# A recurrent layer beside a mixture of experts on one core: another order of the work in each step

## Chip, core and metric

The kernel runs on one NeuronCore of a Trainium2 chip. The metric is the device time of one execution in microseconds (us); lower is better. All data is float32.

## What is computed

`x` holds 32 sequences of 256 tokens with 128 channels, 8192 tokens. Both branches read the same normalised `xn`, and the output joins them:

```python
xn = _layernorm(x, axis=-1)
s = _L0_attn_ref(xn, ...)                 # recurrent branch
g = _silu(_L0_ffn_ref(xn, ...))           # shared expert + one of 8 routed experts
x = x + s * g
```

The recurrent branch is an RWKV layer. Time mixing: layernorm, a blend of each token with the one before it, three products `k`, `v`, `r`, and a recurrence over time with a running maximum:

```python
out = (e1 * aa + e2 * vv) / (e1 * bb + e2)
...
rwkv = sr * _wkv(time_decay, time_first, k, v)
x = x + jnp.einsum('btd,cd->btc', rwkv, att_ow)
h = _ln(x, ln2_w, ln2_b)                  # channel mixing from here
kk = jnp.square(jax.nn.relu(jnp.einsum('btc,fc->btf', xk, f_kw)))
kv = jnp.einsum('btf,cf->btc', kk, f_vw)
x = x + jax.nn.sigmoid(jnp.einsum('btc,dc->btd', xr, f_rw)) * kv
```

The other branch is `silu(x @ wg.T) * (x @ wu.T) @ wd.T` with shared weights for every token, plus the same form with the weights of the token's best expert, applied to `x` times the sigmoid of the best logit.

## The kernel before

Each engine (TensorE, ScalarE, VectorE, GpSimd, and SyncE for transfers) has a program of its own, written out by hand in one order; engines meet at semaphores that count finished instructions. An instruction that waits holds up everything behind it on its engine.

The 8192 tokens are 16 chunks of 512. A prologue loads and normalises all of them, transposes them into `XT` and computes the router's logits. Then come steps 0 to 17. Step `i` works on three chunks: it opens chunk `i+1` (transpose of `z1`, `make_h1`, `make_d1`, `time_mixes`, the products `k`, `v`, `r`, `running_max`, `differences`), does the recurrence of chunk `i` (`decays`, `wkv_b`, `wkv_a`, `den_and_num`, `inverse_of_den`, `make_tn`, `make_rw`), and finishes chunk `i-1` (`attention_out`, `make_x2`, `rstd_of_x2`, `make_z2`, `make_h2`, `channel_mixes`, four `ffn_key` products, relu, square, `ffn_value`, `make_s`). `make_x2` adds the attention output and takes its statistics on VectorE; `rstd_of_x2` makes four instructions of four columns on GpSimd from them; `make_z2` on ScalarE applies them. The inverse of the denominator is `exp(-ln(den + 1))`, and its table of functions is loaded in each step (L735), and the table with tanh and silu again (L749). The square of the keys is made for two quarters on ScalarE and for two on VectorE (L1069). GpSimd makes `rw` (L837).

Between these pieces each step has eight places, `fill(i, 0)` to `fill(i, 7)`, which stand in every engine's order. `plan()` puts other work there:

- `S m q`: half of chunk `m` of the shared expert: two products, silu, a product on VectorE; with `q = 0` also the down product of chunk `m-1`. `D m` is a down product alone.
- `E n`: a slot of the routed experts. A tile has 128 tokens of one expert, and there are 71. Slot `n` does gate and up of tile `n` (8 matmuls, L486), transposes tile `n+2` (1), and does down of tile `n-2` (4, L500). SyncE loads a tile's 384 KB of weights into one of five buffers, when the down product of the tile five before it is done.
- `Z c`: the final part of chunk `c`: add shared and routed rows, silu, times the recurrent branch, plus `x`, store. It needs all experts.

Steps 0 to 5 hold the shared chunks 0 to 13 (step 0 eight halves, the others four each). Before the experts, GpSimd must scatter all 64 tiles of tokens into expert order in DRAM, by indirect transfers: four in step 0 and twelve in each of the steps 1 to 5. Steps 6 to 14 hold the experts, eight slots a step. Step 15 holds Z 0 to 5, step 16 the shared chunks 14 and 15 and Z 6 to 12, and step 17 the last four.

In a step of before, TensorE ends with key 0, key 1, `k`, `v`, key 2, key 3, `r` and the whole value product, so that all of chunk `i-1` ends in step `i`.

## Time and profile before

| | |
|---|---|
| device time, median of 3 | 577.74 us (577.66 to 578.63) |
| the profiled execution | 577.9 us, of which the span of instructions is 576.1 |
| TensorE busy | 464.0 us (81%) |
| VectorE busy | 425.2 us (74%) |
| ScalarE busy | 345.6 us (60%) |
| GpSimd busy | 264.7 us (46%) |
| mean granted TensorE clock | 0.959 |
| `attention_out` of a step starts | 100.0 (step 1), 127.6, 155.9, 183.0, 210.1, 237.2 (step 6), 269.7, 298.2, 327.4, 355.9, 384.7, 413.2, 441.7, 470.4 (step 14), 497.3, 531.8 |

`attention_out` opens a step on TensorE, so that the differences of the last row are the lengths of the steps. In rows of the trace, L12 is line 12 of the kernel, PE is TensorE's matmuls, PEld its weight loads, DVE VectorE, ACT ScalarE, POOL GpSimd and SPq the queue of transfers. Each fp32 matmul of the program stands there as two instructions. `[0.61 <-DMA ...]` is idle time of the engine before the instruction, and what ended it.

### The profile page before, as it was taken

What the parts mean: (1) busy time and instruction counts of PE and PEld (TensorE: products, weight loads), DVE (VectorE), ACT (ScalarE), POOL (GpSimd) and SP (SyncE); (2) the same over time, 40 slices, a digit from 0 to 9 for tenths busy, and PEclk for the clock granted to TensorE, in tenths of its full rate; (3) what the DMA queues carried; (4) which work ended last, traced back from release to release, by engine and by line L of the source; (5) the groups of instructions that cost most, each with busy time, mean ns of one, the idle gap of its engine ahead of it and who ended that gap; (6) DMA issues with size and microseconds to landing.
All of it is one profiled execution on the core that took longest, in us unless ns stands there. A gap on an engine that the chain in (4) does not pass through costs nothing. (4 is left out here: it accounts for less than half of the span.)

```text
span 576.1 us, 8950 instructions
## 1 busy us (share of the span) xinstructions
PE 464.0 (81%) x2623; PEld 345.9 (60%) x2623; DVE 425.2 (74%) x836; ACT 345.6 (60%) x707; POOL 264.7 (46%) x317
## 2 busy tenths in 40 slices
PE   0989777797979797889898989898989897637661
PEld 0989244564646464787777777777777776425341
DVE  3553795879697977695969596969696968783766
ACT  3776423665646566676776677677777676536441
POOL 6664003657575858461818181818181828210100
PEclk9999988999899999999999999999999999957986
DMA  6329404010000001262727282727272825245482
GB/s 200 110 75 257 96 0 155 22 36 26 33 25 33 31 27 38 62 186 73 221 71 211 84 222 73 209 85 220 73 225 71 226 66 167 73 136 158 128 236 73
DMA packets 68864, 64.97 MB, mean 113 GB/s; under 512 B 5952, under 2 KB 57025, under 8 KB 68816
## 3 DMA queue, kind: packets, MB, share of 16 engines
q1 hardware_dynamic: 63344, 54.31, 34.5%
q0 software_dynamic: 4320, 8.53, 4.2%
q10 hardware_dynamic: 1152, 1.56, 0.8%
q8 instruction: 21, 0.34, 0.2%
q14 instruction: 27, 0.22, 0.1%
HBM read 46.86 MB, written 17.97 MB: 113 GB/s over the span
## 5 line engine op out<-in xcount | busy, mean ns | idle before, releaser
L849 POOL DMA_INDIRECT routed_out<-xh,xs x71 | 91.3, 1286 | 30.2 <-ACT xh L689 16.1
L486 PE MATMUL bank_ring<-xh,ew 128*128 128x128 f32 x568 | 78.6, 281 | 19.9 <-DMA ew<-ex_w 9.3
L486 PEld LDWEIGHTS bank_ring<-xh,ew 128*128 128x128 f32 x568 | 68.8, 191 | 26.9 <-ACT xh L689 15.2
L841 POOL DMA_INDIRECT tokens_by_expert<-xn,pos x64 | 67.2, 1051 | 37.0 <-issue 18.5
L1069 DVE TENSOR_TENSOR kk<-rk 128x512 f32<-128x512 f32 x32 | 26.3, 822 | 54.3 <-ACT rk L650 54.3
L689 ACT ACTIVATE xh<-bank_ring 128x256 f32<-128x256 f32 (+1 forms) x75 | 27.8, 371 | 63.4 <-PE bank_ring L500 62.3
L440 PEld LDWEIGHTS bank_out<-fvw,kk 128*128 128x128 f32 x512 | 60.9, 195 | 8.2 <-issue 8.2
L440 PE MATMUL bank_out<-fvw,kk 128*128 128x128 f32 x512 | 60.8, 278 | 0.0
L823 POOL TENSOR_SCALAR x_sm<-x_mv 128x4 f32<-128x4 f32 x16 | 3.8, 235 | 111.8 <-DVE x_mv L1051 111.8
L470 PE MATMUL bank_ring<-xt,sup 128*128 128x512 f32 x64 | 34.9, 628 | 17.5 <-DVE hs L1085 10.6
L837 POOL TENSOR_TENSOR rw<-den_num,lq 128x512 f32<-128x512 f32 x16 | 20.3, 1269 | 53.8 <-issue 46.5
L500 PE MATMUL bank_ring<-ew,hx 128*128 128x128 f32 x284 | 43.5, 276 | 0.7 <-DVE hx L1093 0.7
L449 PEld LDWEIGHTS bank_ring<-sdn,hs 128*128 128x128 f32 x256 | 31.6, 196 | 15.8 <-DVE hs L1085 12.0
L500 PEld LDWEIGHTS bank_ring<-ew,hx 128*128 128x128 f32 x284 | 38.1, 194 | 1.0 <-ACT xh L689 0.9
L1093 DVE TENSOR_TENSOR hx<-px,bank_ring 128x256 f32<-128x256 f32 x71 | 29.0, 408 | 13.1 <-ACT px L692 12.9
L431 PE MATMUL bank_fa<-xk,fkw 128*128 128x512 f32 x64 | 36.4, 653 | 2.3 <-ACT rk L650 2.3
L449 PE MATMUL bank_ring<-sdn,hs 128*128 128x128 f32 x256 | 32.3, 280 | 6.9 <-DVE hs L1085 6.9
L464 PE MATMUL bank_ring<-xt,sup 128*128 128x512 f32 x64 | 34.9, 628 | 2.3 <-ACT tg L668 2.3
L431 PE MATMUL bank_fb<-xk,fkw 128*128 128x512 f32 x64 | 34.3, 617 | 3.0 <-ACT tf L644 3.0
L1085 DVE TENSOR_TENSOR hs<-tg,bank_ring 128x512 f32<-128x512 f32 x32 | 21.7, 679 | 17.5 <-ACT tg L668 11.8
L470 PEld LDWEIGHTS bank_ring<-xt,sup 128*128 128x128 f32 x64 | 11.4, 193 | 38.7 <-DVE hs L1085 18.0
L572 ACT ACTIVATE xn<-xi,nb,rs 128x128 f32<-128x128 f32 x64 | 26.3, 482 | 12.1 <-POOL nb L801 11.9
(139 smaller groups left out, 1124.0 us busy)
## 6 DMA issues: line engine op xcount, KB each, us to landing
ew<-ex_w SPq DMA_DIRECT2D x71, 384.0 KB, 4.0
xi<-x SPq DMA_DIRECT2D x32, 256.0 KB, 3.7
tokens_by_expert<-pad_row SPq DMA_DIRECT2D x1, 4686.0 KB, 21.2
xs<-tokens_by_expert SPq DMA_DIRECT2D x71, 66.0 KB, 3.6
ew<-routed_out SPq DMA_DIRECT2D x16, 256.0 KB, 3.3
out<-xn SPq DMA_DIRECT2D x16, 256.0 KB, 3.2
routed_out<-xh,xs POOLq DMA_INDIRECT x71, 4.1
tokens_by_expert<-xn,pos POOLq DMA_INDIRECT x64, 2.3
```

The lines of the kernel that those rows point to most:

```text
L431: nc.tensor.matmul((FA, FB)[q % 2][:, :], part(FKW, q, P), XK2[:, :], start=True, stop=True)\
L440: last = nc.tensor.matmul(part(BO, j, CH), KK[:, q * CHUNK + j * P:q * CHUNK + (j + 1) * P], part(FVW, q, CH), start=(q + j == 0), stop=(q ...
L449: last = nc.tensor.matmul(part(b, j, CH), h[:, q * CHUNK + j * P:q * CHUNK + (j + 1) * P], part(SDN, q, CH), start=(q == 0), stop=(q == EQ ...
L464: nc.tensor.matmul(ring(5 * m + 3 * q)[:, :], part(SUP, q, P), part(XT, m, CHUNK), start=True, stop=True)\
L470: nc.tensor.matmul(ring(5 * m + 3 * q + 1)[:, :], part(SUP, EQ + q, P), part(XT, m, CHUNK), start=True, stop=True).then_inc(s_su, 1)
L486: last = nc.tensor.matmul(part(GU[n % 2], q, P), part(w, q, P), xt[:, 0:P], start=True, stop=True)
L500: last = nc.tensor.matmul(BX[:, P:P + CH], part(h, q, P), part(w, 2 * EQ + q, CH), start=(q == 0), stop=(q == EQ - 1))
L572: last = nc.scalar.activation(xn_tile(t), part(XI[c % 4], j, P), ACT.Identity, bias=NB[:, t:t + 1], scale=RS[:, t:t + 1])
L689: nc.scalar.activation(XH[n % NXH][:, a:b], BX[:, a:b], ACT.Copy).then_inc(s_xh, 1)
L841: nc.gpsimd.indirect_dma_start(xs_dram, bass.IndirectOffsetOnAxis(ap=POS[:, t:t + 1], axis=0), XN[:, t * XROW:(t + 1) * XROW], None).then_ ...
L849: nc.gpsimd.indirect_dma_start(routed_dram, bass.IndirectOffsetOnAxis(ap=XS[(n - 2) % NXS][:, CH:CH + 1].bitcast(i32), axis=0), XH[n % NXH ...
L1093: nc.vector.tensor_tensor(HX[n % NHX][:, :], PX[n % 2][:, :], GU[n % 2][:, EF:2 * EF], ALU.mult)\
```

## The change

The plan: experts start at step 5 instead of 6, so that they take steps 5 to 13; the shared chunks 12 to 15 come behind them, into steps 14 and 15, and `D 15` into step 16. Z 0 to 3 go into step 14, Z 4 to 9 into step 15, Z 10 to 15 into step 16, and only Z 16 remains for step 17. GpSimd scatters fifteen tiles a step in steps 1 to 4.

```diff
-EARLY, LATE = 14, 16
-E_STEP = 6
+EARLY, LATE = 12, 16
+E_STEP = 5
...
     late = [("S", m, q) for m in range(EARLY, LATE) for q in range(2)] + [("D", LATE - 1, 0)]
-    for k, item in zip((0, 1, 2, 3, 4), late):
-        steps[CHUNKS][k].append(item)
-    for c in range(6):
-        steps[CHUNKS - 1][c + 2].append(("Z", c))
-    for c in range(6, CHUNKS - 3):
-        steps[CHUNKS][c - 6].append(("Z", c))
-    for c in range(CHUNKS - 3, CHUNKS + 1):
-        steps[CHUNKS + 1][0].append(("Z", c))
+    for n, item in enumerate(late):
+        steps[E_STEP + width + n // 4][2 * (n % 4)].append(item)
+    for c in range(CHUNKS):
+        n = c + 2
+        steps[E_STEP + width + n // 6][1 + n % 6].append(("Z", c))
+    steps[CHUNKS + 1][7].append(("Z", CHUNKS))
...
+        TR = [sb(f"tr{u}", CHUNK) for u in range(2)]
+        X2 = [sb(f"x2{u}", CHUNK) for u in range(2)]
+        KB = (FA, FB, FB, FA)
...
             def key_value(c):
...
                     pe.wait_ge(s_n2, c)
+                    pe.wait_ge(s_ev, c)
...
             def ffn_key(c, q):
                 if q == 0:
                     pe.wait_ge(s_mix2, 2 * c + 2)
-                    pe.wait_ge(s_tr, min(c + 2, CHUNKS))
+                    pe.wait_ge(s_tr, min(c + 3, CHUNKS))
                 elif q == 1:
                     pe.wait_ge(s_tf, c + 1)
+                elif q == 2:
+                    pe.wait_ge(s_rk, 4 * c + 2)
                 else:
-                    pe.wait_ge(s_rk, 4 * c + q - 1)
-                nc.tensor.matmul((FA, FB)[q % 2][:, :], part(FKW, q, P), XK2[:, :], start=True, stop=True)\
+                    pe.wait_ge(s_rk, 4 * c + 1)
+                nc.tensor.matmul(KB[q][:, :], part(FKW, q, P), XK2[:, :], start=True, stop=True)\
                   .then_inc(s_fk, 1)
-            def ffn_value(c):
-                if c > 0:
+            def ffn_value(c, a, b):
+                if a == 0 and c > 0:
                     pe.wait_ge(s_u, c)
-                for q in range(FQ):
-                    pe.wait_ge((s_kk, s_kd)[q % 2], 2 * c + 1 + q // 2)
+                for q in range(a, b):
+                    pe.wait_ge(s_kk, 4 * c + 1 + q)
                     for j in range(TPC):
                         last = nc.tensor.matmul(part(BO, j, CH), KK[:, q * CHUNK + j * P:q * CHUNK + (j + 1) * P],
                                                 part(FVW, q, CH), start=(q + j == 0), stop=(q + j == FQ + TPC - 2))
-                last.then_inc(s_kv, 1)
+                if b == FQ:
+                    last.then_inc(s_kv, 1)
```

`X2` and `TR` have two buffers, so that a chunk's channel mixing can end two steps after its recurrence. The keys 0 to 3 use the banks FA, FB, FB, FA instead of FA, FB, FA, FB, and `v` of a chunk waits also for the `ev` of the chunk before it. The value product comes in two halves, around `attention_out`, with keys 2 and 3 ahead of it; keys and value there are of chunk `i-2`. TensorE's step:

```diff
             def step(i):
                 C, P1 = 0 < i <= CHUNKS, i + 1 < CHUNKS
+                if P1:
+                    z1_transpose(i + 1)
+                if i > 1:
+                    ffn_key(i - 2, 2)
+                    ffn_key(i - 2, 3)
+                    ffn_value(i - 2, 0, 2)
                 if C:
                     attention_out(i - 1)
+                if i > 1:
+                    ffn_value(i - 2, 2, FQ)
+                fill(i, 0)
                 if P1:
-                    z1_transpose(i + 1)
-                fill(i, 0)
+                    key_value(i + 1)
+                if C:
+                    z2_transpose(i - 1)
                 fill(i, 1)
+                if P1:
+                    receptance(i + 1)
                 fill(i, 2)
                 if i == 0:
                     routing_prefix()
                 fill(i, 3)
-                fill(i, 4)
-                if C:
-                    z2_transpose(i - 1)
-                fill(i, 5)
-                fill(i, 6)
                 if C:
                     ffn_receptance(i - 1)
+                    ffn_key(i - 1, 0)
+                fill(i, 4)
+                fill(i, 5)
+                if C:
+                    ffn_key(i - 1, 1)
+                fill(i, 6)
                 fill(i, 7)
-                if C:
-                    ffn_key(i - 1, 0)
-                    ffn_key(i - 1, 1)
-                if P1:
-                    key_value(i + 1)
-                if C:
-                    ffn_key(i - 1, 2)
-                    ffn_key(i - 1, 3)
-                if P1:
-                    receptance(i + 1)
-                if C:
-                    ffn_value(i - 1)
```

ScalarE starts a step with a table load and the inverse of chunk `i-1`, and makes all four squares. The scores of the router are made with Ln and Exp instead of Sigmoid:

```diff
-                nc.scalar.activation(rows_of_xn[:, :, CH + 1], MX[:, :], ACT.Sigmoid).then_inc(s_sc, 1)
+                nc.scalar.activation(SC[:, :], MX[:, :], ACT.Exp, scale=-1.0).then_inc(s_sc, 1)
+                act.wait_ge(s_sc, 1)
+                nc.scalar.activation(SC[:, :], SC[:, :], ACT.Ln, bias=CST[:, K_ONE:K_ONE + 1]).then_inc(s_sc, 1)
+                act.wait_ge(s_sc, 2)
+                nc.scalar.activation(rows_of_xn[:, :, CH + 1], SC[:, :], ACT.Exp, scale=-1.0).then_inc(s_sc, 1)
...
             def step(i):
                 C, T, P1 = 0 < i <= CHUNKS, i < CHUNKS, i + 1 < CHUNKS
-                fill(i, 0)
+                if C:
+                    nc.scalar.preload_act_table_set("natural_log_exp_and_others")
+                    inverse_of_den(i - 1)
+                if i > 1:
+                    ffn_relu(i - 2, 2)
+                    ffn_square(i - 2, 2)
                 if P1:
                     make_h1(i + 1)
+                if i > 1:
+                    ffn_relu(i - 2, 3)
+                    ffn_square(i - 2, 3)
                 if T:
-                    tanh_d(i)
-                fill(i, 1)
+                    decays(i)
+                if i == 0:
+                    scores()
+                if i <= CHUNKS:
+                    nc.scalar.preload_act_table_set("silu_and_others")
+                if i == 0:
+                    tanh_d(0)
+                    receptance(0)
                 if C:
                     make_z2(i - 1)
+                fill(i, 0)
+                if C:
+                    make_h2(i - 1)
+                fill(i, 1)
+                if P1:
+                    receptance(i + 1)
                 fill(i, 2)
                 fill(i, 3)
-                if T:
-                    receptance(i)
-                fill(i, 4)
-                if C:
-                    make_h2(i - 1)
-                fill(i, 5)
-                fill(i, 6)
                 if C:
                     ffn_tanh(i - 1)
+                    ffn_relu(i - 1, 0)
+                    ffn_square(i - 1, 0)
+                fill(i, 4)
+                fill(i, 5)
+                if C:
+                    ffn_relu(i - 1, 1)
+                    ffn_square(i - 1, 1)
+                fill(i, 6)
                 fill(i, 7)
-                if T:
-                    nc.scalar.preload_act_table_set("natural_log_exp_and_others")
-                if C:
-                    ffn_relu(i - 1, 0)
-                    ffn_relu(i - 1, 1)
-                    ffn_square(i - 1, 0)
-                if T:
-                    inverse_of_den(i)
-                if C:
-                    ffn_relu(i - 1, 2)
-                    ffn_relu(i - 1, 3)
-                    ffn_square(i - 1, 2)
                 if P1:
-                    decays(i + 1)
-                if T:
-                    nc.scalar.preload_act_table_set("silu_and_others")
+                    tanh_d(i + 1)
```

GpSimd no longer makes `rw`, and does `make_d1` first:

```diff
             def step(i):
                 C, T, P1 = 0 < i <= CHUNKS, i < CHUNKS, i + 1 < CHUNKS
+                if P1:
+                    make_d1(i + 1)
                 if C:
                     rstd_of_x2(i - 1)
-                if P1:
-                    make_d1(i + 1)
-                for k in range(4):
-                    fill(i, k)
+                fill(i, 0)
                 if 0 < i < E_STEP:
-                    scatter(12)
-                for k in range(4, 8):
+                    scatter(15)
+                for k in range(1, 8):
                     fill(i, k)
                 if i == 0:
                     pool.wait_ge(s_fill, 16)
                     pool.wait_ge(s_rt, RT_PLACED)
-                    pool.wait_ge(s_sc, 1)
+                    pool.wait_ge(s_sc, 3)
                     pool.wait_ge(s_tok, 1)
                     scatter(4)
-                if T:
-                    make_rw(i)
```

VectorE makes `rw`, no squares, and takes `make_s` one step later. `differences`, `wkv_b`, `wkv_a` and `den_and_num` are split, with the same instructions, into `difference_of_key` (the `e2` part), `exp_value` (`ev`), `value_of_now` (`N2`) and `weighted_sums`:

```diff
+            def make_rw(c):
+                dve.wait_ge(s_tn, c + 1)
+                dve.wait_ge(s_iq, c + 1)
+                if c > 0:
+                    dve.wait_ge(s_att, c)
+                nc.vector.tensor_tensor(RW[:, :], NUM, LQ[:, :], ALU.mult).then_inc(s_rw, 1)
...
             def step(i):
                 C, T, P1 = 0 < i <= CHUNKS, i < CHUNKS, i + 1 < CHUNKS
+                if T and i > 0:
+                    value_of_now(i)
+                if i + 2 < CHUNKS and i > 0:
+                    make_z1(i + 2)
                 if C:
+                    make_rw(i - 1)
                     make_x2(i - 1)
+                if P1:
+                    time_mixes(i + 1)
+                if T:
+                    exp_value(i)
                 fill(i, 0)
                 if i == 0:
                     routing_counts()
+                    value_of_now(0)
                 if T:
                     wkv_b(i)
-                fill(i, 1)
+                if i > 1:
+                    make_s(i - 2)
                 if T:
                     wkv_a(i)
-                fill(i, 2)
+                fill(i, 1)
                 if i == 0:
                     routing_starts()
+                if C:
+                    channel_mixes(i - 1)
+                fill(i, 2)
+                if T:
+                    weighted_sums(i)
+                fill(i, 3)
+                if i == 0:
+                    routing_rows()
                 if T:
                     den_and_num(i)
-                fill(i, 3)
-                if P1:
-                    time_mixes(i + 1)
-                if i == 0:
-                    routing_rows()
+                    make_tn(i)
                 fill(i, 4)
-                if C:
-                    channel_mixes(i - 1)
-                fill(i, 5)
-                if T:
-                    make_tn(i)
-                fill(i, 6)
-                if i + 2 < CHUNKS:
-                    make_z1(i + 2)
-                fill(i, 7)
-                if C:
-                    ffn_square(i - 1, 1)
                 if P1:
                     running_max(i + 1)
-                if C:
-                    ffn_square(i - 1, 3)
+                fill(i, 5)
                 if P1:
+                    difference_of_key(i + 1)
                     differences(i + 1)
-                if C:
-                    make_s(i - 1)
+                if i == 0:
+                    make_z1(2)
```

## Rows read from the trace of the kernel before

**Rows 1.** Busy time by stretch (each a step, or several), with its columns

```profile
core 0: us, PE busy (x) PEld busy (x) DVE busy (x) ACT busy (x) POOL busy (x), PEclk, DMA share, GB/s
62.00:100.00 38.00, 27.49 (x95) 14.47 (x94) 28.23 (x50) 15.11 (x23) 6.42 (x6) 0.91 0.21 65
...
100.00:127.60 27.60, 24.15 (x119) 15.26 (x120) 22.49 (x36) 16.95 (x29) 16.85 (x18) 1.00 0.09 30
...
210.10:237.20 27.10, 23.83 (x121) 15.11 (x120) 22.68 (x36) 16.09 (x28) 17.80 (x18) 1.00 0.10 31
237.20:269.70 32.50, 28.39 (x200) 23.35 (x198) 22.77 (x41) 24.11 (x56) 13.75 (x13) 1.00 0.48 134
269.70:298.20 28.50, 25.55 (x177) 20.84 (x176) 22.48 (x40) 20.06 (x46) 14.11 (x14) 1.00 0.52 147
...
441.70:470.40 28.70, 25.30 (x176) 20.77 (x175) 22.50 (x40) 20.05 (x46) 14.80 (x14) 1.00 0.51 146
...
497.30:531.80 34.50, 15.30 (x63) 10.24 (x62) 23.08 (x39) 14.68 (x25) 6.01 (x5) 0.65 0.43 123
531.80:576.10 44.30, 23.16 (x110) 14.29 (x108) 30.62 (x54) 15.44 (x28) 2.57 (x4) 0.86 0.49 142
```

**Rows 2.** A line's group: xcount, busy us, mean ns, idle before and releaser

```profile
L1069 DVE TENSOR_TENSOR kk<-rk 128x512 f32<-128x512 f32 x32 | 26.3, 822 | 54.3 <-ACT rk L650 54.3
```

**Rows 3.** Timeline of an expert step, TensorE: start us, length us, instruction

```profile
328.73 1.06 PE L486 MATMUL bank_ring<-xh,ew 128*128 128x128 f32 x8
...
330.18 1.06 PE L486 MATMUL bank_ring<-xh,ew 128*128 128x128 f32 x8
```

**Rows 4.** Timeline, same step: attention sum, scan, normalisation, table load and inverse

```profile
329.11 0.69 DVE L1044 TENSOR_TENSOR x<-bank_fb,xn 128x512 f32<-128x512 f32 x1
...
331.46 0.24 POOL L823 TENSOR_SCALAR x_sm<-x_mv 128x4 f32<-128x4 f32 x1 [7.78 <-DVE x_mv L1051]
...
332.05 1.22 DVE L1012 TENSOR_TENSOR_SCAN bb_aa<-e 128x514 f32<-128x514 f32 x1
...
333.39 1.65 ACT L629 ACTIVATE z<-x,x_sm 128x128 f32<-128x128 f32 x4
...
346.60 1.28 ACT L735 ACT_TABLE_LOAD   x1
...
349.39 0.72 ACT L620 ACTIVATE lq<-den_num,consts 128x512 f32<-128x512 f32 x1
...
350.14 0.63 ACT L622 ACTIVATE lq<-lq 128x512 f32<-128x512 f32 x1
```

**Rows 5.** Timeline of a shared step, VectorE and GpSimd side by side

```profile
207.27 2.17 DVE L1000 SCALAR_TENSOR_TENSOR e<-pp,vectors 128x512 f32<-128x512 f32 x1
...
207.60 1.28 POOL L837 TENSOR_TENSOR rw<-den_num,lq 128x512 f32<-128x512 f32 x1
209.36 0.73 DVE L1004 SCALAR_TENSOR_TENSOR dd<-pp,vectors,bank_k 128x512 f32<-128x512 f32 x1
```

**Rows 6.** Timeline near the end, VectorE and GpSimd side by side

```profile
536.07 0.68 DVE L1100 TENSOR_TENSOR xn<-xt,xn 128x512 f32<-128x512 f32 x1
536.12 0.72 POOL L824 TENSOR_SCALAR x_sm<-x_mv 128x4 f32<-128x4 f32 x1
```

**Rows 7.** Timeline of the expert step, slots on TensorE and waits for weights

```profile
329.74 0.61 PE L500 MATMUL bank_ring<-ew,hx 128*128 128x128 f32 x4
...
331.18 0.61 PE L500 MATMUL bank_ring<-ew,hx 128*128 128x128 f32 x4
...
334.23 1.13 PE L486 MATMUL bank_ring<-xh,ew 128*128 128x128 f32 x8 [0.61 <-DMA ew<-ex_w]
...
336.82 1.13 PE L486 MATMUL bank_ring<-xh,ew 128*128 128x128 f32 x8 [0.68 <-DMA ew<-ex_w]
```

**Rows 8.** Timeline of step 0: the routing scans, and a slow matmul

```profile
66.92 3.25 DVE L942 TENSOR_TENSOR_SCAN kk<-consts,kk 128x64 f32<-128x64 f32 x8
...
83.73 1.91 PE L464 MATMUL bank_ring<-xt,sup 128*128 128x512 f32 x2
```

81 lines of the change are left out of this document (39 added, 42 removed).

## Prediction

> **What bounds the kernel now.** I read the busy table by stretch first. Before step 1 lie 62 us of prologue and 38 of step 0; then come five shared steps (27.1 us each but for 28.3 once and 27.6 in the first), a first expert step of 32.5, seven of 28.5 to 29.2 that make 200.7 together, one of 26.9, and 78.8 us for steps 15 to 17 [rows 1]. The reader is to see three things. In an expert step TensorE is busy for 25.6 of 28.5 us, VectorE for 22.5 and ScalarE for 20.1: no engine is full, and TensorE has at most 3 us to give. In step 15 TensorE is busy for 15.3 of 34.5 us, and its granted clock is 0.65 [rows 1]. And VectorE stands idle for 54.3 us ahead of its 32 squares, waiting for ScalarE's relu [rows 2]. So before, the end of a step is a chain of key, relu, square and value product on which everything waits. The change cuts it in two and lays it over two steps. What counts is whether another chain then sets the length of a step, since the work itself hardly changes.
>
> **What is added and removed.** VectorE loses two squares a step (2 x 0.82) [rows 2] and gets `rw`, an operation of the size of `make_x2`'s sum, 0.69 [rows 4]. A GpSimd operation that runs beside VectorE costs it more than its own time: with `rw` on GpSimd from 207.60 to 208.88, VectorE's `e` took 2.17, and its next operation of the same kind and size 0.73 [rows 5]. That goes too. ScalarE gets two squares, some 2 x 0.6, and has 8 us free. GpSimd loses `rw` (1.28) [rows 5] and gets three scatters a step, by estimate 4 us; in a shared step it is busy for 17.8 of 27.1 us [rows 1]. Its scatters stand behind `rstd_of_x2` and ahead of the next `make_d1`, which is needed only 8 us into the step. Engine time thus costs nothing. Order does.
>
> **The new chain of a shared step.** I count from the end of `differences` in the step before. ScalarE makes tanh (0.63), loads the table (1.28), makes Ln and Exp (349.39 to 350.77, 1.4 with the wait between) [rows 4]: 3.35. `rw` 0.69, `attention_out` 1.2: 5.25. From the start of the x2 sum to GpSimd's first instruction 2.35 (329.11 to 331.46): 7.6. GpSimd's four instructions took 1.9 (to 333.39) [rows 4]. All of this used to lie beside other work; now VectorE has in it only `N2`, `z1`, `time_mixes` and `ev`, some 4.2 us, and waits.
>
> Here an uncertain price decides. Before, nothing that reads two SBUF operands stood beside those four instructions for long. In the new order the three `time_mixes` start right as they do. In a stretch where VectorE did have such work, GpSimd's second instruction took 0.72, until VectorE's operation ended, not its usual 0.23 [rows 6]. With three mixes of 0.66 and one held up by each, GpSimd ends at 10.6; if mixes hold nobody up, at 9.5. I take 10.6, since these operands are both in SBUF, as those in the row. The Trainium skill (SBUF, State Buffer, "SBUF: two separate sides") has the rule: a VectorE operation with two SBUF inputs and a GpSimd operation that reads SBUF share a port pair under an exclusive lock, and the later one waits. Here it speaks against the change, and the row agrees with it (0.72 for 0.23); by the rule the step is the 26.65 below, without it 25.55.
>
> Then `make_z2` 1.65 [rows 4] and silu 0.6, both ahead of VectorE's first fill since ScalarE's order is fixed: VectorE resumes at 12.8. Behind that stands the rest of its step: 22.68 busy in a shared step before [rows 1], less 1.64 (squares) and 1.44 (the lengthened `e`, 2.17 - 0.73) [rows 5], plus 0.69, less what was done already (8 operations of 0.69, 1.3 for the statistics, 6.8) gives 13.5, and with some 0.35 of gaps 13.85. Sum: 12.8 + 13.85 = 26.65 against 27.1.
>
> **An expert step**, from TensorE's first instruction. ScalarE ends its three small operations of the last slot and tanh at 1.65 (an estimate, 1.0 and 0.63), the inverse at 4.35 (1.28 and 1.4), `rw` 5.05, `attention_out` 6.25, GpSimd starts at 8.6 and, held up, ends at 11.6; z2 13.2; silu of the first slot 13.85; VectorE's product 14.3. Then `wkv_b` (1.2), `make_s` (1.4), `wkv_a` (1.2) [rows 4] and the second product: 18.3, on which TensorE's fourth slot waits. From there it is full: a slot costs 1.45 (328.73 to 330.18) [rows 3], five of them 7.25, `ffn_receptance` 0.9 and two keys 1.7 (8 and 2 x 8 pieces of 128 columns, at 1.45 / 13 each): 28.2. Weights can be late once more: from the end of a slot to the start of the third after it TensorE needed 3.9 us when it waited (330.35 to 334.23) and 5.0 the next time (331.79 to 336.82) [rows 7]. In the new order such a gap is 3.76 (two slots and a key) in one place of the step, so 0.1 to 1.2 are lost; I take 0.2, as the shorter of the two, for the queue is then less crowded. 28.4 against a mean of 28.67 (200.7 / 7).
>
> **Step 0.** `v` of chunk 1 now waits in TensorE's queue for `N2` of chunk 0, which stands behind the eight routing scans (3.25 us from 66.92) [rows 8], and with it every shared half behind. Before, `v` was near the end of the step. I estimate that step 0 ends 1.5 to 5.5 us later; TensorE slowed down after such a gap before: a pair with 2 x 512 columns took 1.91 there [rows 8], and eight with 128 columns, the same number, 1.06 in the expert step [rows 3]. I take 3.5. The sigmoid's own table load (1.28) falls away.
>
> **The end.** Before, the sixth shared step and steps 15 to 17 (27.1 + 78.8) [rows 1] take 105.9. After: step 14 is a shared step with four Z, each some 1.85 on VectorE (three operations of 0.69, overlapped), without `z1`: 26.65 + 7.4 - 0.6 = 33.45. Step 15 has six Z (11.1) but no mixes, `running_max` or `differences`, and its last Z stands ahead of the table load on ScalarE: 32.7. Steps 16 and 17: attention, channel mixing and both halves of the value product of chunk 15 in series, six Z between them: 37. Together 103.15.
>
> **Sum**, against the profiled execution's 577.9 (1.8 over its span, 0.16 over the median of 577.74): step 0 +3.5; step 1 (no `make_s`) 25.3 for 27.6, -2.3; steps 2 to 4 80.0 for 82.5, -2.5; first expert step, with its empty pipeline (4.0 over the others before, 4.4 now behind z2) 32.8 for 32.5, +0.3; seven expert steps 198.8 for 200.7, -1.9; the last one 0; the end -2.75. That is -5.65: **572.2 us**.
>
> **Rivals.**
>
> *GpSimd isn't held up.* The mixes have a scalar as a third operand, unlike the operation of the row. Then 1.1 less in each of fourteen steps: 557. For it: in the expert step the four took 1.9 though a scan began beside them at 332.05 [rows 4]. Against: the scan began after them, and the mixes begin before.
>
> *Weights become late in earnest (the other side).* Each slot's weights need 5.0 us instead of 3.9, as in the second wait [rows 7]. Then 1.0 more in each of eight expert steps: 580. It turns the sign from 0.7 a step. For it: seven of eight slots now run in pairs, with nothing between. Against: TensorE's long head of the step gives the queue 8 us to catch up.
>
> *The end gives nothing.* With its clock at 0.65 there before, TensorE may run steps 16 and 17 at the lower level throughout, some 5 us; then 577, no change.
>
> **Numbers.** The forecast has 0.45 (its own range 567 to 577), GpSimd free 0.2, late weights 0.22, no gain at the end 0.13. The range 556 to 582 reaches into both outer rivals. 0.2% is about what a measurement of this kernel can tell. Faster by more: most of the forecast, all of the first rival, a third of the last: 0.65; slower: the late weights and part of the last and of the forecast, 0.27; the rest, 0.08, is the same.
>
> **What would show it.** Right: no wait of VectorE for relu; its longest waits ahead of `rw`, the x2 sum and the first product of a step; GpSimd's second and third instruction lengthened to some 0.6 and 1.6 in every step; expert steps of 28.4 and shared ones of 26.6; some waits for weights at one place in a step. Wrong: expert steps under 27.5 (no lock), or over 29 with waits for weights or, what I didn't count, stalls between slots on ScalarE, whose order is now fuller; or a step 0 that ends over 105.

## Result: 1.7% slower, and the profile after

| | median us | ratio to before on the same chip |
|---|---|---|
| before | 578.18 (577.66 to 579.81) | |
| after | 587.63 (587.08 to 590.46) | 1.0168, 95% interval 1.0129 to 1.0208 |

The prediction was 572.2 with a range to 582: wrong in sign and outside the range. The profiled execution took 587.2, of which 585.4 is the span, 9.3 more than before. The busy time by stretch of the changed kernel, for [rows 1]; a step now starts with the transpose of `z1`. The row from 129.80 is steps 2 to 4, the one to 448.30 the seven expert steps behind the first:

```profile
61.50:103.50 42.00, 28.58 (x96) 14.87 (x96) 26.64 (x49) 12.18 (x22) 5.46 (x5) 0.84 0.16 54
103.50:129.80 26.30, 20.94 (x84) 12.36 (x82) 19.56 (x34) 15.24 (x26) 15.42 (x15) 0.87 0.07 24
129.80:211.40 81.60, 72.19 (x354) 47.24 (x355) 62.46 (x105) 52.31 (x87) 62.79 (x63) 0.98 0.12 40
211.40:246.40 35.00, 29.62 (x198) 24.95 (x198) 21.78 (x40) 23.98 (x55) 13.44 (x15) 0.95 0.35 102
...
246.40:448.30 201.90, 177.10 (x1221) 144.07 (x1220) 147.09 (x273) 151.25 (x329) 97.65 (x92) 1.00 0.49 146
448.30:476.20 27.90, 23.28 (x157) 18.36 (x156) 20.57 (x38) 19.85 (x43) 13.70 (x13) 1.00 0.44 129
476.20:510.30 34.10, 27.75 (x122) 16.89 (x122) 26.06 (x44) 19.21 (x34) 5.72 (x7) 0.95 0.30 86
510.30:546.80 36.50, 24.91 (x104) 17.27 (x105) 25.52 (x44) 19.13 (x34) 1.66 (x4) 0.81 0.44 124
546.80:585.40 38.60, 21.71 (x98) 16.03 (x96) 20.55 (x38) 18.32 (x30) 1.66 (x4) 0.72 0.37 108
```

Against before, in us:

| stretch | before | predicted change | measured change |
|---|---|---|---|
| up to step 1 | 100.0 | +3.5 | +3.5 |
| step 1 | 27.6 | -2.3 | -1.3 |
| steps 2 to 4 | 82.5 | -2.5 | -0.9 |
| first expert step | 32.5 | +0.3 | +2.5 |
| seven expert steps | 200.7 | -1.9 | +1.2 |
| last expert step | 26.9 | 0 | +1.0 |
| the end, from step 14 on | 105.9 | -2.75 | +3.3 |
| sum | 576.1 | -5.65 | +9.3 |

No single stretch explains it: each term but the first came out too low, the end by 6 us.

The stall that the change was to remove is gone: VectorE has no squares, and no wait for relu [rows 2]. Two groups of the page show what took its place (xcount, busy us, mean ns, idle before, releaser). VectorE's product in an expert slot stood idle for 13.1 us before; now:

```profile
L1110 DVE TENSOR_TENSOR hx<-px,bank_ring 128x256 f32<-128x256 f32 x71 | 29.4, 413 | 44.9 <-ACT px L701 44.5
...
L638 ACT ACTIVATE z<-x,x_sm 128x128 f32<-128x128 f32 x64 | 26.4, 482 | 39.1 <-POOL x_sm L842 39.1
```

The head of an expert step, in the timeline of the changed kernel, for [rows 4]. The step opens at 332.65:

```profile
337.11 0.69 DVE L1060 TENSOR_TENSOR rw<-den_num,lq 128x512 f32<-128x512 f32 x1 [1.46 <-issue]
...
339.05 0.69 DVE L1067 TENSOR_TENSOR x<-bank_fb,xn 128x512 f32<-128x512 f32 x1 [1.25 <-PE bank_fb L409]
...
341.09 0.72 DVE L988 SCALAR_TENSOR_TENSOR xk<-d,vectors,h 128x512 f32<-128x512 f32 x1
341.40 0.51 POOL L836 TENSOR_SCALAR x_sm<-x_mv 128x4 f32<-128x4 f32 x1 [1.44 <-DVE x_mv L1074]
341.73 0.75 DVE L988 SCALAR_TENSOR_TENSOR xv<-d,vectors,h 128x512 f32<-128x512 f32 x1
...
341.99 0.57 POOL L837 TENSOR_SCALAR x_sm<-x_mv 128x4 f32<-128x4 f32 x1
...
342.53 1.51 POOL L839 TENSOR_TENSOR x_sm<-x_sm,minus_half 128x4 f32<-128x4 f32 x1
...
346.64 0.42 DVE L1110 TENSOR_TENSOR hx<-px,bank_ring 128x256 f32<-128x256 f32 x1 [2.90 <-ACT px L701]
```

GpSimd's instructions are held up by the mixes as forecast: 0.51, 0.57 and 1.51 us. VectorE idles for 1.46, 1.25 and 2.90 us in this head, where it used to have other work.

### The profile page after: what moved, and what is told of

Read it like the earlier page. It is cut to its first block, busy times and chain, and to the rows that moved or that the text cites. A ratio compares the mean times of both kernels' runs of the same rounds, so it can differ in the third digit from the quotient of the medians.

```text
span 585.4 us, 8964 instructions
## 1 busy us (share of the span) xinstructions
PE 472.8 (81%) x2623; PEld 354.4 (61%) x2623; DVE 400.1 (68%) x820; ACT 368.1 (63%) x740; POOL 251.3 (43%) x301
## 4 chain that ended last, share of the span: by engine, by line
PE 36%; DVE 25%; ACT 14%; issue 13%; POOL 8%; DMA 2%; DVEq 0%; SPq 0%; POOLq 0%; ACTq 0%
PE bank_ring L490 9%; PE bank_ring L504 4%; POOL x_sm L839 4%; ACT z L638 4%; PE bank_fb L409 4%; ACT L724 2%; PE bank_out L443 2%; PE bank_fa L434 2%; PE bank_fb L434 2%; DVE x_bs L1070 2%; DMA xi<-x 2%; DVE bb_aa L1021 2%; DVE x L1067 2%; PE bank_fb L421 2%; DVE hs L1102 2%
## 5 line engine op out<-in xcount | busy, mean ns | idle before, releaser
L847 POOL DMA_INDIRECT tokens_by_expert<-xn,pos x64 | 70.7, 1105 | 47.5 <-DVE kk L969 27.3
L490 PEld LDWEIGHTS bank_ring<-xh,ew 128*128 128x128 f32 x568 | 72.5, 195 | 22.3 <-issue 14.0
L443 PEld LDWEIGHTS bank_out<-fvw,kk 128*128 128x128 f32 x512 | 66.3, 203 | 12.4 <-issue 8.2
L443 PE MATMUL bank_out<-fvw,kk 128*128 128x128 f32 x512 | 69.8, 289 | 1.7
L638 ACT ACTIVATE z<-x,x_sm 128x128 f32<-128x128 f32 x64 | 26.4, 482 | 39.1 <-POOL x_sm L842 39.1
L836 POOL TENSOR_SCALAR x_sm<-x_mv 128x4 f32<-128x4 f32 x16 | 7.6, 473 | 87.6 <-DVE x_mv L1074 87.6
L667 ACT ACTIVATE kk<-rk 128x512 f32<-128x512 f32 x64 | 40.3, 630 | 2.0
L828 POOL TENSOR_TENSOR d<-h 128x512 f32<-128x512 f32 x16 | 16.6, 1039 | 56.7 <-ACT h L604 56.6
L409 PE MATMUL bank_fb<-att,rw 128*128 128x128 f32 x128 | 21.3, 317 | 19.8 <-DVE rw L1060 19.8
L421 PE MATMUL bank_fb<-att,xr 128*128 128x128 f32 x128 | 19.9, 305 | 20.7 <-DVE xr L1085 20.7
```

Of the source, the lines that this page charges most:

```text
L409: last = nc.tensor.matmul(part(FB, j, CH), part(RW, j, P), part(ATT, 3, CH), start=True, stop=True)
L443: last = nc.tensor.matmul(part(BO, j, CH), KK[:, q * CHUNK + j * P:q * CHUNK + (j + 1) * P], part(FVW, q, CH), start=(q + j == 0), stop=(q ...
L490: last = nc.tensor.matmul(part(GU[n % 2], q, P), part(w, q, P), xt[:, 0:P], start=True, stop=True)
L638: nc.scalar.activation(part(Z2, j, P), part(X2[c % 2], j, P), ACT.Identity, bias=SM2[:, 2 * TPC + j:2 * TPC + j + 1], scale=SM2[:, TPC + j ...
L667: nc.scalar.activation(part(KK, q, CHUNK), part(RK, q % 2, CHUNK), ACT.Square).then_inc(s_kk, 1)
L847: nc.gpsimd.indirect_dma_start(xs_dram, bass.IndirectOffsetOnAxis(ap=POS[:, t:t + 1], axis=0), XN[:, t * XROW:(t + 1) * XROW], None).then_ ...
```

## The experiments

Sixteen kernels ran in four groups, each on a chip of its own. The kernel before took 584.0 us there in the first group (`e1` to `e4`), 583.1 in the second (`c_after`, `e7` to `e9`), 578.7 in the third (`b_before`, `e10` to `e12`) and 581.8 in the fourth (`g1` to `g4`), so that ratios within a group are compared. The result above is from a fifth chip, "the first" below. In the expectations, A is the theory that the order of a step makes the loss, B that the plan does.

**1. Order or plan.** `e1`: the step of before with the new plan and fifteen scatters. `e2`: the new step with the plan of before and twelve; the final parts of step 17 stand at its last place.

```diff
-EARLY, LATE = 12, 16
-E_STEP = 5
+EARLY, LATE = 14, 16
+E_STEP = 6
...
-                    scatter(15)
+                    scatter(12)
```

> The order of the kernel before, with the plan of the change alone: experts from step 5, fifteen scatters a step, shared chunks 12 to 15 in steps 14 and 15, the final parts spread over steps 14 to 17. Theory A (the new order costs the time, through a longer chain at the head of each step): the plan alone is no loss. Its steps stay at 27.1 and 28.7, the shared halves fill step 15, and the end takes some 6 us less than before: 572, and at most 577. Theory B (the plan costs it: the first expert step has to wait for the scatters, and the final parts hold up the attention of the last chunks): 583 or more.

> The order of the change with the plan of before: experts from step 6, twelve scatters a step, shared chunks 14 and 15 in step 16, final parts in steps 15 to 17 (those of step 17 behind the last recurrent sum, since one of them needs it). Theory A: as slow as the changed kernel or slower, 586 to 592, since its steps of 28.8 and 27 stay and step 0 stays long. Theory B: 578 or less, since what made it slow is gone.

Measured: `e1` 1.0269 (1.0192 to 1.0346), `e2` 1.0029 (1.0003 to 1.0055). That points to the plan, but `e1` is no clean witness: in the old step `rw` stands behind GpSimd's scatters, and its shared steps grew from 27.1 to between 30 and 35 us; late completions as in experiment 3 stand in its trace too. So the pair was run again in the last group, new order with either plan:

> The changed kernel, beside the kernel before and the new order alone on one chip. 1.0145 to 1.0168 of before, as twice already. The distance to the next kernel is the price of the plan alone, on one chip and in one group.

> The new order of a step with the plan of the kernel before (as the second experiment). Theory A (the order alone makes the loss, the plan gives and costs nothing): the same as the changed kernel within 0.3%. Theory B (the plan makes the loss): 1.003 of before as in the second experiment, that is 7 us under the changed kernel. From the traces, step by step, I expect between them: the same shared and expert steps, and an end 2 to 3 us shorter, so 1.010.

Measured: after 1.0176 (1.0131 to 1.022), order alone 1.0067 (1.0028 to 1.0105). In this group both cost: the medians of the fast runs are 581.79 before, 586.25 with the order alone and 591.25 with both, so 4.5 us for the order and 5.0 for the plan; by the ratios, which go by means, it is 0.7% and 1.1%. Neither theory is right as it stood. The first chip can't be split in this way, since the new order with the old plan didn't run there. The stretches of `e2`, as in the table above: step 1, steps 2 to 5, first expert step, seven more, the last, the end behind it:

```profile
103.40:128.80 25.40, 18.57 (x83) 10.72 (x82) 19.51 (x34) 15.27 (x26) 15.37 (x15) 1.00 0.08 25
128.80:240.10 111.30, 98.70 (x473) 64.32 (x474) 83.36 (x140) 69.71 (x116) 71.43 (x71) 0.95 0.10 32
240.10:275.10 35.00, 29.92 (x198) 25.39 (x198) 21.79 (x40) 24.21 (x55) 10.31 (x11) 0.90 0.31 87
275.10:477.60 202.50, 176.87 (x1221) 144.02 (x1220) 147.47 (x273) 151.28 (x329) 98.33 (x92) 1.00 0.50 147
477.60:504.40 26.80, 22.54 (x152) 17.78 (x150) 19.04 (x36) 19.54 (x41) 13.80 (x13) 1.00 0.45 132
504.40:584.10 79.70, 47.80 (x208) 30.85 (x208) 53.29 (x93) 39.83 (x67) 5.28 (x10) 0.76 0.50 145
```

Beside the traces of the first chip this shows where the new order loses, but not how much: step 0 is 3.4 longer than before, the shared steps 0.5 shorter (136.7 for 137.2), the first expert step 2.5 longer, the seven 1.8, the last 0.1 shorter, the end 0.9 longer (79.7 for 78.8), 8.0 in all. On its own chip the same kernel is only 2.1 us slower than the kernel before (586.08 and 584.01), so that such a sum over two chips is no price. That the steps of `e2` and of the changed kernel are alike (202.5 and 201.9 us for the seven expert steps, 35.0 for the first in both) says that the losses of these steps come with the order, and not with the plan.

**2. The head of the step.** `e3` puts ScalarE's first fill ahead of `make_z2`, so that VectorE's product is released sooner:

```diff
+                fill(i, 0)
                 if C:
                     make_z2(i - 1)
-                fill(i, 0)
-                if C:
                     make_h2(i - 1)
```

`e4` orders VectorE's head so that what reads PSUM comes first, and the mixes, with two SBUF operands, behind GpSimd's first instructions:

```diff
-                if T and i > 0:
-                    value_of_now(i)
                 if i + 2 < CHUNKS and i > 0:
                     make_z1(i + 2)
                 if C:
                     make_rw(i - 1)
                     make_x2(i - 1)
-                if P1:
-                    time_mixes(i + 1)
                 if T:
                     exp_value(i)
+                if T and i > 0:
+                    value_of_now(i)
+                if P1:
+                    time_mixes(i + 1)
```

> The changed kernel, with one move: on ScalarE the first place of a step (fill 0) comes ahead of make_z2. In the changed kernel VectorE stands idle for 2.9 us in an expert step until ScalarE has made z2 and then the first slot's silu. Theory A1 (that order on ScalarE is the whole loss at the head): VectorE goes on 2.9 us earlier, expert steps of 26.5, in all some 560. Theory A2 (GpSimd, held up by VectorE's operations on two SBUF operands, sets the head): VectorE's scan now starts beside GpSimd's last instruction and holds it, z2 and its transpose come some 1 us later on TensorE, and an expert step stays at 28.8; only the shared steps gain some 0.8: 583.

> The changed kernel, with one move: on VectorE ev and N2, which read a PSUM bank, stand between make_x2 and time_mixes, so that GpSimd's four instructions run beside them and not beside the three mixes. Theory A2 (the lock between VectorE and GpSimd costs 1.1 us a step): the four take 1.9 to 2.3 instead of 3.0 us, z2 starts 0.8 earlier, and each of fourteen steps is some 0.8 shorter: 576. Theory A1 or any in which the lock is hidden: the four get shorter, but the steps stay at 28.8 and 27.0: 586.

Measured: `e3` 1.0246 (1.0191 to 1.0301), `e4` 0.9973 (0.9942 to 1.0004). `e3` failed. VectorE, released sooner, started its scan as GpSimd began its last instruction, which took 1.28 us for 0.20, and `z2` was later, not sooner (6.45 us behind the start of the x2 sum in the rows below, 5.37 in the rows of the changed kernel). Its expert steps took 30.7 us (214.7 / 7), at a granted clock of 0.95 for 1.00; neither theory had that:

```profile
171.65 1.28 POOL L841 TENSOR_TENSOR x_sm<-x_sm 128x4 f32<-128x4 f32 x1
171.70 1.23 DVE L1020 TENSOR_TENSOR_SCAN bb_aa<-e 128x514 f32<-128x514 f32 x1
...
172.96 1.65 ACT L638 ACTIVATE z<-x,x_sm 128x128 f32<-128x128 f32 x4 [3.07 <-POOL x_sm L841]
...
174.66 1.11 PE L415 MATMUL bank_fb<-consts,z 128*128 128x128 f32 x4 [2.22 <-ACT z L638]
```

`e4` held. GpSimd's first three instructions took 0.23, 0.23 and 1.04; its fourth, now beside the mixes, took 0.63 for 0.20, so that the four need 2.3 us for 3.0. VectorE's wait for its product fell from 2.90 to 1.65, and an expert step took 28.2 us (197.6 / 7) where it takes 28.9 in `e2` on the same chip:

```profile
343.06 0.66 DVE L1017 TENSOR_TENSOR ev<-e,bank_v 128x512 f32<-128x512 f32 x1
343.37 0.23 POOL L836 TENSOR_SCALAR x_sm<-x_mv 128x4 f32<-128x4 f32 x1 [1.45 <-DVE x_mv L1074]
343.63 0.68 DVE L1028 SCALAR_TENSOR_TENSOR tanh_d_and_value<-tanh_d_and_value,bank_v 128x512 f32<-128x512 f32 x1
343.68 0.23 POOL L837 TENSOR_SCALAR x_sm<-x_mv 128x4 f32<-128x4 f32 x1
343.88 1.04 POOL L839 TENSOR_TENSOR x_sm<-x_sm,minus_half 128x4 f32<-128x4 f32 x1
344.23 0.75 DVE L988 SCALAR_TENSOR_TENSOR xk<-d,vectors,h 128x512 f32<-128x512 f32 x1
...
347.95 0.42 DVE L1110 TENSOR_TENSOR hx<-px,bank_ring 128x256 f32<-128x256 f32 x1 [1.65 <-ACT px L701]
```

`e7` and `e8` have the edit of `e4` and `N2` of step 0 ahead of the routing scans, `e7` with the plan of before, `e8` with the new one. `c_after` is the changed kernel in that group.

```diff
+                    value_of_now(0)
                     routing_counts()
-                    value_of_now(0)
```

> The changed kernel itself, once more, beside the kernel before and the other three kernels of this group on one chip, so that all of them can be compared. On the first chip it was 1.0168 of the kernel before. If the chips differ only in a scale, it is 1.017 here too. If it is under 1.010 or over 1.022, the size of the loss hangs on the chip, and small differences between kernels of different groups say nothing.

> New order of a step, plan of the kernel before with twelve scatters, and on VectorE z1, rw, the x2 sum and its statistics, ev and N2 ahead of the three time mixes, so that no operation with two SBUF operands stands beside the first of GpSimd's four small instructions; in step 0 N2 ahead of the routing scans. Theory L (the lock costs the head of each step 0.7 to 1.1 us): 14 steps at 0.7 less and 3 in step 0 less than the new order with this plan, so 1.003 - 0.022 = 0.981 of before, about 10 us faster. Theory M (the steps are bound elsewhere, by TensorE's slots and late weights, and a shorter head is given back later): 1.000 or more, expert steps stay at 28.8.

> The changed kernel with the same two moves on VectorE (PSUM readers ahead of the time mixes; N2 of step 0 ahead of the routing scans), plan untouched. Theory L: 13 us (2.2%) under the changed kernel on the same chip, about 0.995 of before. Against the same moves with the old plan it shows the price of the plan alone: theory D says 5 us (0.9%) or more; if the plan costs nothing, the two are equal within 0.3%.

Measured: `c_after` 1.0145 (1.0099 to 1.0191), `e7` 0.9812 (0.9768 to 0.9857), `e8` 0.9936 (0.9908 to 0.9964). Theory L holds: 13.3 us between `c_after` and `e8` (592.64 and 579.34), 13 forecast. That the total fits so well is in part luck. `N2` early gave more than the 3 us of the forecast in `e8`: step 1 opens at 98.2 there and at 100.6 in `e7`, but at 103.7 in `c_after`, on the same chip. The seven expert steps gave 4.2 (202.5 to 198.3), 0.6 each for 0.7. The group also prices the plan on its own, which the expectation asked for: with the same order `e8` is 6.6 us slower than `e7` (579.34 and 572.78), 1.2% of before. Theory D, 5 us or more, holds. So the plan cost on both chips on which it was tried apart.

`e10` takes GpSimd out of the head of `e7`: ScalarE makes the reciprocal deviation ahead of its table load.

```diff
+                act.wait_ge(s_sm2, c + 1)
...
+                nc.scalar.activation(SM2[:, TPC:2 * TPC], SM2[:, 0:TPC], ACT.Ln).then_inc(s_rs2, 1)
+                act.wait_ge(s_rs2, 2 * c + 1)
+                nc.scalar.activation(SM2[:, TPC:2 * TPC], SM2[:, TPC:2 * TPC], ACT.Exp, scale=-0.5).then_inc(s_rs2, 1)
```

> The order with PSUM readers first and the plan of the kernel before, but GpSimd's four small instructions are gone: VectorE adds epsilon to the variance (0.1 us), ScalarE makes exp(-0.5 ln) of four columns ahead of the load of the silu table, VectorE makes the bias. Theory H (the serial head of a step from tanh to the first product of the fill sets its length): from the x2 sum to z2 4.2 us instead of 5.0, so 0.8 less in 16 steps, 560 to 563 where the same kernel with GpSimd took 572.8 of 583.1, that is 0.96 to 0.965 of before. Theory T (TensorE's own work and late weights set it by now): 0.98 as without the edit.

Measured: 0.9732 (0.97 to 0.9765), 562.89 us for 578.73. That is 0.8% less than `e7` where 1.5 to 2 were forecast, and theory H explains it only in part. From the x2 sum to the first product of an expert step it took 6.55 us for 6.93 in `e4`, 0.4 less and not 0.8, for ScalarE's table load now waits for the statistics; an expert step is 27.9 us (195.0 / 7) for 28.1 in `e7`. The shared steps 2 to 5 fell by more, from 109.0 us together in `e7` to 102.9 (25.7 each), and the first expert step from 35.3 to 32.0. There the granted clock changed too: 0.94, 0.94, 1.00, 0.94 and 0.90 in these five steps of `e7`, 1.00 in all of `e10`. TensorE stands idle for 1.81 us ahead of `ffn_receptance` in a shared step of `e10`, whose eight instructions then take 1.16; in `e7` it is 2.18 to 2.46 us, and they take 1.81, 2.08, 1.16 and 1.27. `e11`, on the chip of `e10`, looks like `e7` (27.7 and 27.5 us at a clock of 0.94, 26.3 at 1.00, first expert step 35.2 at 0.90). How much of the gain is the shorter chain and how much the clock that it kept up, no run separates. VectorE's idle time before `hx` is 23.9 us in all. The rows are steps 2 to 5, the first expert step and the seven behind it:

```profile
123.30:226.20 102.90, 94.38 (x473) 61.61 (x474) 85.06 (x149) 72.39 (x125) 58.02 (x52) 1.00 0.10 33
226.20:258.20 32.00, 27.70 (x197) 23.18 (x198) 22.07 (x42) 24.06 (x56) 7.17 (x7) 1.00 0.37 102
258.20:453.20 195.00, 175.74 (x1220) 145.70 (x1220) 149.42 (x287) 154.59 (x343) 76.75 (x64) 1.00 0.51 151
```

With the plan of before, this order and its short head are worth some 16 us.

**3. Fifteen scatters.** `e9`: `e2` with `scatter(15)` in steps 1 to 4 and none in step 5. `e12`: `e7` with one wait more, on the channel mixes, ahead of its twelve.

```diff
                 if 0 < i < E_STEP:
+                    pool.wait_ge(s_mix2, 2 * i)
                     scatter(12)
```

> New order of a step, plan of the kernel before (experts from step 6, its end), but fifteen scatters a step in steps 1 to 4 and none in step 5. The new order with twelve scatters and this plan was 1.003 of before. Theory C (fifteen scatters a step are what costs: shared steps grow, landing of the scatters or GpSimd's queue is late): 1.010 or more, and shared steps 1 to 4 about 1 us longer each than 27. Theory D (the placing of final parts and late shared chunks in steps 14 to 16 costs): the same as with twelve scatters, 1.003 within 0.003, and shared steps 1 to 4 of 25.4 to 28, as in the changed kernel.

> PSUM readers first, plan of before with twelve scatters a step (0.981 of before), but GpSimd waits for the channel mixes before it starts a step's scatters, so that they reach into the head of the next step, as fifteen do. Theory P (scatters that are issued while TensorE has its transposes, keys 2 and 3 and the value product are what makes TensorE's completions late by 1.5 to 3 us): late completions appear in steps 1 to 5 and the shared steps grow by 0.5 to 1.5 us each, 0.985 to 0.99 of before. Theory N (it is the number of scatters): no late completion, 0.981.

> The kernel before itself with a profile on this chip. On the chip of the first profile its time was 577.7 us; on the chips of the other experiments it was 583.1 and 584.0. If the chips differ by a scale, every step is 1% longer here. If single stretches differ, they show as waits or as late completions in some steps only.

Measured: `e9` 1.0106 (1.0055 to 1.0157), `e12` 1.0121 (1.009 to 1.0152), before against itself 1.0004 (0.9978 to 1.003). By time `e9` speaks for theory C, but weakly: its kernel with twelve scatters took 1.0029 on one chip and 1.0067 (1.0028 to 1.0105) on another, and the second interval overlaps that of `e9`. Only its time is used. `c_after`, of the same group, shows one thing that happens there: in step 2 VectorE waits for the attention output 2.9 us longer than in the changed kernel's first trace, though by the model of their ends TensorE's eight instructions are done at 134.3 (133.10 and 1.16). First `c_after`, then the changed kernel in its first trace:

```profile
132.36 0.69 DVE L1060 TENSOR_TENSOR rw<-den_num,lq 128x512 f32<-128x512 f32 x1 [1.46 <-issue]
137.16 0.69 DVE L1067 TENSOR_TENSOR x<-bank_fb,xn 128x512 f32<-128x512 f32 x1 [4.12 <-remote]
```

```profile
133.09 0.69 DVE L1060 TENSOR_TENSOR rw<-den_num,lq 128x512 f32<-128x512 f32 x1 [1.46 <-issue]
135.03 0.69 DVE L1067 TENSOR_TENSOR x<-bank_fb,xn 128x512 f32<-128x512 f32 x1 [1.25 <-PE bank_fb L409]
```

The records of semaphores put TensorE's update 2.9 us behind the end of its matmuls there. Such lags over 1 us stand in the shared steps with fifteen scatters of `c_after`, `e4` and `e8`, four to nine in a trace (1.0 to 3.0 us), and of `e3`, there up to 4.4. How many they are depends on how updates are matched, for on these chips the traces lack 42 to 70 of TensorE's some 450 records of updates, and on the other two at most one. The waits don't hang on that: the x2 sum did start later. `e2` and `e7`, with twelve, have none. On the first chip, and on the third group's (`b_before`, `e10`, `e11`, `e12`), there is none at all, with fifteen either, and in the fourth group `g2`, with twelve, has 29, and `g1` and `g4`, with fifteen, two each. So a plain count is not the cause, and `e12` can't decide between P and N: it has no lag, but neither has any kernel on its chip. The shared steps of `e12` behind the first are 29.5 to 30.7 for another reason: `make_d1` and the four small instructions now stand behind scatters. The cause of the lags stays open; what the traces show is that they come on some chips and not on others.

**4. The end.** `e11`: `e8` with each final part one place earlier.

```diff
-        steps[E_STEP + width + n // 6][1 + n % 6].append(("Z", c))
+        steps[E_STEP + width + n // 6][n % 6].append(("Z", c))
```

> The changed kernel with PSUM readers first (0.9936 of before), but each final part in steps 14 to 16 one place earlier, so that none stands at the place just ahead of the table load of the next step. Theory E (the last final part's silu on ScalarE and sums on VectorE hold up tanh, the table load and the inverse of the next step): 2 to 3 us less, 0.989 of before. Theory F (VectorE's work and the serial chains of the end set it, wherever the final parts stand): within 1 us of 0.9936.

Measured: 0.9941 (0.9915 to 0.9967), as `e8` (0.9936): theory F. Moving the final parts by one place doesn't give the time back; other plans of the end weren't tried.

**5. The first expert step.** In it TensorE stands idle while ScalarE makes `z2` and scales the first rows, and then needs 1.91 us for what took 1.06. The changed kernel:

```profile
222.29 1.65 ACT L638 ACTIVATE z<-x,x_sm 128x128 f32<-128x128 f32 x4 [2.09 <-POOL x_sm L842]
...
224.32 0.97 ACT L684 ACTIVATE xs<-xs 128x128 f32<-128x128 f32 x3
224.86 0.30 PE L497 MATMUL bank_ring<-consts,xs 128*128 128x128 f32 x1 [4.00 <-ACT xs L684]
...
225.79 1.91 PE L490 MATMUL bank_ring<-xh,ew 128*128 128x128 f32 x8
...
227.71 1.65 PE L490 MATMUL bank_ring<-xh,ew 128*128 128x128 f32 x8
```

`g1` puts the last shared rows and `scale_rows` ahead of `make_z2` in that step (and leaves them out where they stood); `g2` does so in `e10`.

```diff
+                if i == E_STEP:
+                    shared_out(EARLY - 1)
+                    for t in range(3):
+                        scale_rows(t)
                 if C:
                     make_z2(i - 1)
```

> The changed kernel, but in the first expert step ScalarE copies the last shared rows and scales the first three tiles of tokens ahead of make_z2 instead of behind it. Theory G (in that step TensorE stands idle for 4.0 us behind z2, and drops to its lower clock for the slots after it): the wait falls to some 2 us, the slots take 1.06 and not 1.91 and 1.65, and the step is 2 to 2.5 us shorter than its 35.0; 0.004 less of before than the changed kernel. Rival: the x2 chain is now a microsecond later in that step and takes it back, no difference.

> The fastest kernel so far (0.973 of before: PSUM readers first, reciprocal deviation on ScalarE, plan of before) with the same move in the first expert step. Its first expert step is 33.2 us against 27.8 of the others. Theory G: 1.5 to 2 us less there, 0.970 of before. Rival: nothing, 0.973.

Measured: `g1` 1.0124 (1.009 to 1.0157) beside 1.0176 for the changed kernel, `g2` 0.9715 (0.9691 to 0.9739). The step fell from 36.1 us in `g4` to 33.5 in `g1`, 2.6 less; the intervals of the ratios overlap, so that the step is shown and the total only likely. Some 1.5 of them are the order: from the start of `attention_out` to the first slot it took 8.7 us (220.41 to 229.10) for 10.2 in `g4` (220.22 to 230.43). Some 0.9 are the clock, which came back sooner: from the first slot to the product of `v` it took 4.1 us for 5.0, the second slot 1.35 for 1.92, and the granted clock of the step was 0.95 for 0.91. The first slot was as slow as before, against theory G, and TensorE's idle time came in two pieces. The rows are of `g1`:

```profile
226.60 0.30 PE L497 MATMUL bank_ring<-consts,xs 128*128 128x128 f32 x1 [1.07 <-ACT xs L684]
...
228.84 0.47 PE L497 MATMUL bank_ring<-consts,xs 128*128 128x128 f32 x1 [1.93 <-ACT xh L695]
229.10 1.91 PE L490 MATMUL bank_ring<-xh,ew 128*128 128x128 f32 x8
...
231.02 1.35 PE L490 MATMUL bank_ring<-xh,ew 128*128 128x128 f32 x8
```

In `g2` the move shows no gain: the ratio is that of `e10` within the intervals, and the first expert step took 33.2 us, at a clock of 0.95, where it took 32.0 at 1.00 in `e10`.

## Why the prediction was wrong

- **Step 0** (+3.5 forecast and measured): right, by the mechanism named. Moving `N2` ahead of the scans took back 3.1 us in `e7` and 5.5 in `e8`, so that the exact figure is partly luck; it was the middle of an estimate of 1.5 to 5.5.
- **The new chain.** Right, and close. From the start of an expert step to the end of the second product I had 18.3 (the terms add up to 18.5); it is 18.3 (332.65 to 350.95). GpSimd's four instructions took 3.0 us, as forecast. By the Trainium skill (SBUF, State Buffer, "SBUF: two separate sides") the lock between operations of VectorE with two SBUF inputs and GpSimd was to hold them up; the trace agrees, with 0.51 and 0.57 for 0.23, and so does `e4`, with 0.23 beside operations that read PSUM.
- **Expert steps** (28.4 forecast, 28.84 measured): the step "from there it is full" failed. The 0.2 for late weights didn't come (the trace has no wait of TensorE for weights over 0.15 us, where before had 9.3 us of them), and 0.6 was lost that the terms left no room for: among it, the fourth slot starts 0.15 us behind the copy and the product that it waits for, and the last slot of each of the seven has a second wait, of 0.1 to 0.57. That is small, but the whole forecast gain there was 0.27 a step. The last expert step, which I took over unchanged, has the same head and lost 1.0.
- **First expert step** (+0.3 forecast, +2.5 measured): "4.4 now behind z2" failed. It made the step 0.4 longer over the others than before, and 2.2 came (35.0 is 6.2 over them). The last shared copy and the first scaled rows stand behind `z2` as well, TensorE waits 4.00 us where it waited 1.07, and then eight instructions take 1.91 and 1.65 for 1.06, a cost of the clock that the sum put at nothing. `g1` got 2.6 us back, some 1.5 by the order and 0.9 by the clock.
- **Shared steps** (26.65 forecast, 27.2 measured in steps 2 to 4): the sum was nearly right and left out the clock. From the end of `differences` to VectorE's first product it took 13.25, 12.92 and 12.92 us for 12.8, and from there to the end of `differences` 13.84, 13.84 and 14.85 for 13.85. The 1.0 us by which step 4 is longer is TensorE's: idle for 2.84 us, it needed 2.08 for `ffn_receptance`, at a granted clock of 0.94 in this step, and VectorE's next product waited 0.93. In step 2 the same idle time had no such effect:

```profile
148.58 1.16 PE L421 MATMUL bank_fb<-att,xr 128*128 128x128 f32 x8 [2.92 <-DVE xr L1085]
...
202.09 2.08 PE L421 MATMUL bank_fb<-att,xr 128*128 128x128 f32 x8 [2.84 <-DVE xr L1085]
```

- **The end** (-2.75 forecast, +3.3 measured) is the largest miss. Step 14 took 34.1 for 33.45; step 15 36.5 for 32.7; steps 16 and 17 38.6 for 37. In step 15 the term "but no mixes" failed. I took the mixes, some 2 us, off the length, though by my own chain they stand in the head, where VectorE waits anyway: from its opening to VectorE's first product the step took 12.6 us (510.3 to 522.89), where step 3 with its mixes took 12.7 (156.9 to 169.64). GpSimd was free in it (0.23, 0.23, 1.04 and 0.20), but at a TensorE clock of 0.81 the attention output took 2.08 for 1.16. The other 2 us are waits of VectorE for the silu of later products, 0.36 and 1.73. `e11` shows that one place earlier for the final parts gives nothing back. For steps 14, 16 and 17 no run shows which term failed; what a better plan of the end would give wasn't tried. Step 15 on VectorE:

```profile
513.61 0.69 DVE L1060 TENSOR_TENSOR rw<-den_num,lq 128x512 f32<-128x512 f32 x1 [2.06 <-ACT lq L631]
516.47 0.69 DVE L1067 TENSOR_TENSOR x<-bank_fb,xn 128x512 f32<-128x512 f32 x1 [2.17 <-PE bank_fb L409]
...
522.89 0.69 DVE L1102 TENSOR_TENSOR hs<-tg,bank_ring 128x512 f32<-128x512 f32 x1 [3.73 <-ACT tg L677]
...
544.78 0.69 DVE L1102 TENSOR_TENSOR hs<-tg,bank_ring 128x512 f32<-128x512 f32 x1 [1.73 <-ACT tg L677]
```

- **The rivals.** GpSimd was held up, so the first is out. Weights didn't become late, so the second is out. The last, "the end gives nothing", had the right place, but 577 was still too low. The mistake they share: I let the loss of one stage be the mirror of the gain of another, and had no rival in which every stage came out half a microsecond longer. A step of 28 us in which three engines hand on some twenty times loses at many places what a sum of durations leaves out, and no term behind step 0 had what TensorE's clock costs after an idle time.

So the change removed a 54 us wait of one engine and built a serial head of 14 us into each step, in which that engine idles again. That the head sets the length of an expert step is shown: with 0.7 us less in it (7.59 to 6.93 from the x2 sum to the first product) such a step is 0.7 shorter. The plan costs 5.0 to 6.6 us by itself where it was tried apart; why, and how the 9.3 us of the first chip divide, stays open. With the plan of before and the short head the kernel is 2.7% faster than before.

## What to carry to other kernels

When a wait is taken away by another order, write down the new order's serial chain and shorten it in the same change; here, on one chip, the changed kernel was 1.5% slower than before with one order of VectorE's head and 0.6% faster with another (`N2` of step 0 moved as well), and with the old plan 1.9% faster. Here it paid to put operations that read PSUM beside short GpSimd instructions (0.23 us each), and those with two SBUF operands (0.51 and 0.57) behind them. Test the two halves of a change apart: this one had an order and a plan, and the plan was a loss. Where a forecast rests on gains of 1% a step, the gaps between instructions are of the same size, and the range has to hold them.

## What the runs showed of the hardware

TensorE's semaphore updates can come 1 to 3 us, and up to 4.4 (in `e3`), behind the end of its matmuls, while GpSimd issues indirect transfers; on two of five chips no trace shows one. In those groups the kernel before took 577.7 to 579.1 us, in the other three 581.8 to 584.0. That the same lags make the difference is a guess, as before wasn't profiled there.

TensorE's granted clock can fall after an idle time of 2 to 3 us, and need not. Ahead of `ffn_receptance` in shared steps, an idle time of 1.81 us left it at 1.00 in all four steps of `e10`; after 2.84 to 2.92 us the eight instructions took 1.16, 1.16 and 2.08 us in the changed kernel.

VectorE, released sooner, can slow the instruction of GpSimd that its own next input waits for. In the shared steps of `e3` a scan whose start is recorded 0.05 us behind that of a GpSimd instruction of 0.20 us stretched it to 1.28; in the expert steps, where the scan starts 0.2 us ahead, it took 1.01. In both the two end together.
